# Attention probabilities turned by a DMA, and s_j laid along the rows through memory: a graph network on one core

## What is computed

```python
h = jnp.maximum(_layernorm(x, axis=-1), 0.0)
mask = adj + eye > 0
for l in range(3):
    si = h @ attn_w[l, :d]
    sj = h @ attn_w[l, d:]
    scores = si[:, :, None] + sj[:, None, :] + attn_b[l]
    scores = jnp.where(scores >= 0, scores, 0.2 * scores)
    scores = jnp.where(mask, scores, -jnp.inf)
    attn = jax.nn.softmax(scores, axis=-1)
    agg = jnp.einsum('bij,bjd->bid', attn, h)
    r = layernorm(h + agg, g1[l], beta1[l])
    ff = jax.nn.gelu(r @ W1[l] + b1[l], approximate=False) @ W2[l] + b2[l]
    h = layernorm(r + ff, g2[l], beta2[l])
out = x + h
```

## Time and profile before

| what | value |
|---|---|
| runs | 2316.35, 2315.44, 2313.62 us |
| median | 2315.44 us |
| the profiled execution | 2317.27 us, span 2315.5 us |
| PE busy | 2247.7 us, 97% of the span |
| PE weight loads busy | 1575.8 us, 68% |
| DVE busy | 1793.1 us, 77% |
| ACT busy | 1905.2 us, 82% |
| POOL busy | 1872.8 us, 81% |
| DMA, SP's queue | 101.37 MB, 19.3% of 16 engines |
| granted TensorE clock, mean | 0.992 |

### The profile page before, as it was taken

The page is one execution under the profiler, slowest core; times in us unless marked ns, Lnnn a source line. Parts: engine busy times, 40 slices in busy tenths (PEclk is TensorE's granted clock), DMA queues, the critical chain, the costliest instruction groups (busy, mean ns, idle before and its releaser), DMA issues.

```text
span 2315.5 us, 46432 instructions
## 1 busy us (share of the span) xinstructions
PE 2247.7 (97%) x15840; PEld 1575.8 (68%) x15840; DVE 1793.1 (77%) x5887; ACT 1905.2 (82%) x3496; POOL 1872.8 (81%) x1642
## 2 busy tenths in 40 slices
PE   4899999999999999999999999999999999999998
PEld 3666777776667677777666767777766677777675
DVE  7677777778887777777888877777888877777765
ACT  6778888888888888888888888888888888888874
POOL 6467877888988787878898878787989887878786
PEclk9899999999999999999999999999999999999999
DMA  6321111124442111112443111111443211111133
GB/s 180 91 65 28 24 24 24 24 42 83 96 105 47 20 28 19 29 21 53 101 100 88 33 20 28 19 29 19 83 105 88 46 24 24 26 22 28 38 69 78
DMA packets 279273, 120.06 MB, mean 52 GB/s; under 512 B 209792, under 2 KB 277376, under 8 KB 279040
## 3 DMA queue, kind: packets, MB, share of 16 engines
q1 hardware_dynamic: 263200, 101.37, 19.3%
q0 software_dynamic: 15840, 15.73, 4.6%
HBM read 49.96 MB, written 16.78 MB: 29 GB/s over the span
## 4 chain that ended last, share of the span: by engine, by line
PE 75%; DVE 12%; ACT 8%; issue 3%; DMA 1%; POOL 1%; SPq 0%; DVEq 0%; POOLq 0%; ACTq 0%
PE p_hid L417 34%; PE p_pair L431 33%; PE p_pair L477 4%; DVE g_lo L645 2%; DVE bn L652 2%; PE p_pair L455 2%; ACT probs L566 2%; PE p_pair L463 1%; DVE res L728 1%; ACT p_hid L531 1%; ACT L531 1%; DVE res L749 1%; ACT L566 1%; ACT g_hi L536 1%; DVE adj_in L673 1%
## 5 line engine op out<-in xcount | busy, mean ns | idle before, releaser
L645 DVE TENSOR_TENSOR g_lo<-p_hid,g_hi 128x512 f16<-128x512 f32 x768 | 529.9, 690 | 475.7 <-ACT g_hi L536 469.2
L431 PE MATMUL p_pair<-w_hi,g_hi 128*128 128x256 f16 x3072 | 837.9, 273 | 0.0
L431 PE MATMUL p_pair<-w_lo,g_hi 128*128 128x256 f16 x3072 | 837.8, 273 | 0.0
L431 PE MATMUL p_pair<-w_hi,g_lo 128*128 128x256 f16 x3072 | 837.8, 273 | 0.0
L531 ACT ACTIVATE p_hid<-p_hid,b_eff 128x512 f32<-128x512 f32 x768 | 505.5, 658 | 310.0 <-PE p_hid L417 308.3
L897 POOL TENSOR_TENSOR rstd<-var_eps,minus_half 128x4 f32<-128x4 f32 x224 | 236.6, 1056 | 382.9 <-DVE minus_mean L660 382.8
L536 ACT ACTIVATE g_hi<-p_hid 128x512 f16<-128x512 f32 x768 | 459.3, 598 | 24.5
L417 PE MATMUL p_hid<-hT_hi,w_hi 128*128 128x512 f16 x1536 | 458.2, 380 | 6.5 <-DMA hT_hi<-h_hi 3.5
L417 PE MATMUL p_hid<-hT_lo,w_hi 128*128 128x512 f16 x1536 | 458.7, 380 | 0.9 <-DMA hT_lo<-h_lo 0.8
L417 PE MATMUL p_hid<-hT_hi,w_lo 128*128 128x512 f16 x1536 | 458.6, 380 | 0.0
L431 PEld LDWEIGHTS p_pair<-w_lo,g_hi 128*128 128x128 f16 x3072 | 300.8, 98 | 106.7 <-issue 0.3
(11 more groups left out here) (73 smaller groups left out, 3520.2 us busy)
## 6 DMA issues: line engine op xcount, KB each, us to landing
x_in<-in_x SPq DMA_DIRECT2D x32, 512.0 KB, 3.8
out<-w_f SPq DMA_DIRECT2D x31, 512.0 KB, 5.0
w_f<-in_x POOLq DMA_DIRECT2D x30, 512.0 KB, 6.1
adj_in<-in_adj SPq DMA_DIRECT2D x32, 256.0 KB, 4.4
...
hT_hi<-h_hi SPq DMA_TRANSPOSE x96, 3.1
hT_lo<-h_lo SPq DMA_TRANSPOSE x96, 3.1
...
```

Of the source, the lines that this page charges most:

```text
L431: mm = pe.matmul(ff_banks(s)[:, t, :], g[i][:, nodes], w[l][:, c, :], start=(c == 0 and t % 2 == 0 and n == 0), stop=(c == C - 1 and n == ...
L645: dve.tensor_tensor(g_lo[i][:], p_hid[k][:], g_hi[i][:], ALU.subtract).then_inc(g_lo_ready, 1)
```

## The change

- `transpose_probs` and `copy_probs` go. ACT makes p_hi, a float16 copy of the probabilities, in SBUF; DVE makes p_lo = probs - p_hi, in SBUF; two DMA transposes on SP's queue write pT_hi and pT_lo.
- `spread_sj` on PE stays for the first four items only. From item 4 on SP writes s_j to a small DRAM buffer (`sj_to_memory`) and reads it back, repeated over the 128 partitions, as sj_rows in SBUF (`sj_to_rows`). The scores read sj_rows in place of the PSUM bank.
- The order in the slot changes on every engine: on DVE p_lo goes from chunk 4 to chunk 0, the feed residual from 2 to 1, its statistics from 3 to 2, the scores from 4 to 3, the attention residual from 7 to 5, the dots from 5 to 6, the mask from 6 to 7. ACT's exponentials go from 5 to 6 and the copy p_hi stands in 7. On POOL the norm after the feed moves to the slot after, before the layer's output. The folds for layers 1 and 2 stand as halves in chunks 3 and 4 of slots 1 and 3. Opening and loads of x are rearranged, and there is one more slot at the end.

```diff
+        sj_rows = sb("sj_rows", [P, T, N])
+        sj_memory = [nc.dram_tensor(f"sj_memory{i}", [T, N], F32).ap() for i in range(2)]
...
-        pT_hi, pT_lo = sb("pT_hi", [P, TN], F16), sb("pT_lo", [P, TN], F16)
+        p_hi, p_lo = sb("p_hi", [P, T, N], F16), sb("p_lo", [P, T, N], F16)
+        pT_hi, pT_lo = sb("pT_hi", [P, T, N], F16), sb("pT_lo", [P, T, N], F16)
...
+            def turn_probs_hi(r, s):
+                sp.wait_ge(p_hi_ready, total(r, s, 1, 1))
+                if later(r, s):
+                    sp.wait_ge(agg_ready, total(r, s - 1, 1, 1))
+                sp.dma_start_transpose(pT_hi[:], p_hi[:].rearrange("p t n -> p (t n)")).then_inc(pT_hi_ready, 16)
...
+            def sj_to_memory(r, s):
+                sp.wait_ge(dots_ready, total(r, s, 8, 8))
+                if later(r, s, 6):
+                    sp.wait_ge(sj_in, sj_total(r, s - 2))
+                with nc.allow_non_contiguous_dma("four bytes of each node and graph"):
+                    sp.dma_start(sj_memory[s % 2].rearrange("t n -> n t"), s_j[s % RING][:]).then_inc(sj_out, 16)
+
+            def sj_to_rows(r, s):
+                sp.wait_ge(sj_out, sj_total(r, s))
+                if later(r, s, 5):
+                    sp.wait_ge(score_steps, total(r, s - 1, 5, 4))
+                sp.dma_start(sj_rows[:].rearrange("p t n -> p (t n)"),
+                             sj_memory[s % 2].rearrange("t n -> (t n)").partition_broadcast(P)).then_inc(sj_in, 16)
...
-                    if c == 4 and is_item(r, s + 2):
-                        transpose_probs(r, s + 2)
+                    if c == 6 and is_item(r, s + 2):
+                        aggregate(r, s + 2)
                     if c < LAG and is_item(r, s - 1):
                         feed(r, s - 1, C - LAG + c)
                     if c >= LAG and is_item(r, s):
                         feed(r, s, c - LAG)
 
-                    if c == 3 and is_item(r, s + 3):
-                        spread_sj(r, s + 3)
-                    if c == 6 and is_item(r, s + 2):
-                        aggregate(r, s + 2)
...
-            def copy_probs(r, s):
-                act.wait_ge(pT_psum, total(r, s, 1, 1))
-                act.activation(pT_hi[:].rearrange("p (t n) -> p t n", n=N), pT_bank(s), ACT.Copy).then_inc(pT_hi_ready, 1)
+            def high_probs(r, s):
+                act.wait_ge(probs_ready, total(r, s, 4, 4))
+                if later(r, s):
+                    act.wait_ge(pT_hi_ready, total(r, s - 1, 16, 16))
+                act.activation(p_hi[:], probs[:], ACT.Copy).then_inc(p_hi_ready, 1)
...
             def add_scores(r, s):
                 q = s % RING
-                dve.wait_ge(sj_rows_ready, total(r, s, 1, 1))
+                first = isinstance(r, int) and r == 0 and s < 4
+                if first:
+                    dve.wait_ge(sj_rows_ready, s + 1)
+                else:
+                    dve.wait_ge(sj_in, sj_total(r, s))
+                rows = sj_bank(s) if first else sj_rows
                 dve.wait_ge(dots_ready, total(r, s, 8, 8))
                 if later(r, s):
                     dve.wait_ge(leaky_ready, total(r, s - 1, 2, 2))
                 for t in range(T):
-                    dve.scalar_tensor_tensor(out=scores[:, t, :], in0=sj_bank(s)[:, t, :], scalar=s_i[q][:, t:t + 1],
+                    dve.scalar_tensor_tensor(out=scores[:, t, :], in0=rows[:, t, :], scalar=s_i[q][:, t:t + 1],
                                              in1=mask[q][:, t, :], op0=ALU.add, op1=ALU.add).then_inc(score_steps, 1)
...
             def low_probs(r, s):
-                dve.wait_ge(pT_hi_ready, total(r, s, 1, 1))
-                dve.tensor_tensor(pT_lo[:].rearrange("p (t n) -> p t n", n=N), pT_bank(s),
-                                  pT_hi[:].rearrange("p (t n) -> p t n", n=N), ALU.subtract).then_inc(pT_lo_ready, 1)
+                dve.wait_ge(p_hi_ready, total(r, s, 1, 1))
+                if later(r, s):
+                    dve.wait_ge(pT_lo_ready, total(r, s - 1, 16, 16))
+                dve.tensor_tensor(p_lo[:], probs[:], p_hi[:], ALU.subtract).then_inc(p_lo_ready, 1)
...
-                if is_item(r, s - 2):
-
+
+                if is_item(r, s - 2) and not (isinstance(r, int) and (r, s) == (LOOPS, PER + 1)):
+                    norm_feed(r, s - 2)
                     layer_output(r, s - 2)
```

More of the change, by code:

```diff
@@ L55 @@
 LOOPS = ITEMS // PER - 1
[L56 removed]
+FOLD_AT = {4: 1, 6: 2}
 def layer_of(s):
@@ L131, in slots @@
             slot(r, s)
-    for s in range(FIRST_LOOP_SLOT, PER + 1):
+    for s in range(FIRST_LOOP_SLOT, PER + 2):
         slot(LOOPS, s)
@@ L285, in gnn_kernel, with sj_total, x_source @@
         pieces = [(l, n) for l in range(L) for n in range(4)]
-        act_pieces = dict(zip([(s, c) for s in range(4) for c in (0, 1)], pieces[4:]))
-        dve_pieces = dict(zip([(s, c) for s in range(3) for c in (5, 6)] + [(3, 2), (3, 3)], pieces[4:]))
+        act_pieces = dict(zip([(0, 6), (0, 7), (1, 0), (1, 3), (2, 0), (2, 3), (3, 0), (3, 3)], pieces[4:]))
+        dve_pieces = dict(zip([(0, 7), (1, 1), (1, 4), (2, 1), (2, 4), (2, 7), (3, 1), (3, 4)], pieces[4:]))
+        def sj_total(r, s):
+            return total(r, s, 16, 16 - 4 * 16)
+        def x_source(r, s):
+            return X[s] if isinstance(r, int) and r == 0 and s in (2, 3) else x_in[s % 2]
         block = ctx.enter_context(nc.Block())
@@ L317, in store, with turn_h_hi @@
                 sp.dma_start(graphs(out, g), y_out[g % 2]).then_inc(stored[g % 2], 16)
-            def turn_h(r, s):
-                i = s % 2
+            def turn_h_hi(r, s):
                 if later(r, s, 2):
                     sp.wait_ge(hid_psum, total(r, s - 2, C, C))
-                for h, hT, made, turned in ((h_hi, hT_hi, h_hi_ready, hT_hi_ready), (h_lo, hT_lo, h_lo_ready, hT_lo_ready)):
-                    sp.wait_ge(made, total(r, s, 1, 1))
-                    sp.dma_start_transpose(hT[i][:].rearrange("p t k n -> p (t k) n"),
-                                           h[:].rearrange("p t d -> p (t d)")).then_inc(turned, 16)
@@ L328, in slot, with turn_h_lo @@
-            def slot(r, s):
+                sp.wait_ge(h_hi_ready, total(r, s, 1, 1))
+                sp.dma_start_transpose(hT_hi[s % 2][:].rearrange("p t k n -> p (t k) n"),
+                                       h_hi[:].rearrange("p t d -> p (t d)")).then_inc(hT_hi_ready, 16)
+            def turn_h_lo(r, s):
+                sp.wait_ge(h_lo_ready, total(r, s, 1, 1))
+                sp.dma_start_transpose(hT_lo[s % 2][:].rearrange("p t k n -> p (t k) n"),
+                                       h_lo[:].rearrange("p t d -> p (t d)")).then_inc(hT_lo_ready, 16)
@@ new lines, in slot @@
+            def slot(r, s):
+                if is_item(r, s + 2):
+                    turn_probs_hi(r, s + 2)
+                if is_item(r, s + 3) and s >= 1:
+                    sj_to_rows(r, s + 3)
+                if is_item(r, s + 2):
+                    turn_probs_lo(r, s + 2)
+                if is_item(r, s + 3) and layer_of(s + 3) == 0 and group_of(r, s + 3) + 2 < G:
+                    sp.wait_ge(mask_steps, group_total(r, s + 3, 2, 2))
+                    load_adj(group_of(r, s + 3) + 2)
+                if is_item(r, s - 3) and layer_of(s - 3) == L - 1 and not (isinstance(r, int) and (r, s) == (LOOPS, PER + 1)):
+                    store(r, s - 3)
+                if is_item(r, s + 1):
+                    turn_h_hi(r, s + 1)
@@ L434, in feed, with fold_bias @@
                 mm.then_inc(ff_done, 1)
-            def fold_bias(l, bank):
+            def fold_bias(l, bank, half):
                 pe.wait_ge(w_dma[0], 16 * (l + 1))
                 pe.wait_ge(cols_dma, 2 * 16)
-                for c in range(C):
+                for c in range(C // 2 * half, C // 2 * (half + 1)):
                     for k in range(KD):
@@ L976, in slot @@
                     h_residual(r, s + 1)
-                if is_item(r, s - 1):
-                    inverse_deviation(s - 1, 2, total(r, s - 1, 10, 10), total(r, s - 1, 2, 1))
-                    if not (isinstance(r, int) and (r, s) == (LOOPS, PER)):
-                        norm_feed(r, s - 1)
             def first_deviation(i, n):
```

252 lines of the change are left out of this document (133 added, 119 removed).

## The result

The changed kernel takes **2567.5 us** (median of 4 runs, 2564.3 to 2571.0), the kernel before 2314.7 on the same chip: a ratio of 1.109, with a 95% interval of 1.108 to 1.111. It is slower, as forecast, but by 253 us and not by 160: 92 us beyond the forecast's 2475 and 27 beyond the end of the range. The profiled execution has a span of 2569.2 us.

What follows compares the result with a forecast made beforehand. TensorE's instruction list bounded the kernel before; after, VectorE's scores alternating with GpSimd make slots 24.9 us against TensorE's 22.2. Opening 169.6 + slots 2292 + end 13.5 = 2475 us; range 2210 to 2540, the likeliest case's own 2420 to 2540.

Steps and rivals of the forecast that it cites:

- What goes: On TensorE, both transposes leave, 2 x 0.44 = 0.87 us a slot, for a floor of 22.2 us.
- I take 4 ... and 3.1 for the read back. ... Cost 0: SP's queue: s_j's write 4 us and read back 3.1, back at 15.1 before scores start at 15.8; cost 0.
- The alternation: VectorE's two-SBUF-input scores take turns with GpSimd's h_lo and both h_res, one whole instruction each; slot 24.9 us against 22.2.
- The layer-0 slots, 25.4: 24 slots where VectorE also takes input statistics and the mask, which waits 0.95 and 1.1 us; 25.4 us each.
- The rival "s_j late": s_j's transfers end late, each us beyond 15.8 costing 1 us a slot; at 7.8 twice, 2624 us; chance 6%.
- TensorE stays the bound: Rival: VectorE passes the four short scores in one go; 2223 us, or 2257 if layer-0 slots wait; chance 28%.
- The moves priced at 0: p_hi replaces the copy pT_hi on ScalarE; norm_feed fills GpSimd's 4.12 us wait one slot later; each cost 0.
- The opening and the end: Opening left at 169.6 us, give or take 10; end 13.5: three feeds 3.9 and 9.6 from the last feed residual.
- p_lo about 1 us: Sign expected in the profile after: VectorE's p_lo, with both inputs in SBUF, takes about 1 us.
- The turned probabilities hidden: DMA turns of p_hi and p_lo cost nothing: p_lo ready about 9.6 us into VectorE's slot, read some 11 us later.

Runs made afterwards that it cites:

- e11_one_input: e4_wide with GpSimd's h_lo and both h_res as same-size instructions with one SBUF input, part of the result left out; 2251.4 us, 0.972 of the kernel before.
- e10_act_copy: e4_wide with ScalarE copying sj_rows into PSUM for the scores and the mask ahead of the attention residual; 2281.4 us, 0.985 of the kernel before.
- e12_mask_stats: e10_act_copy with the layer-0 items' mask made behind the attention residual and its statistics; 2232.6 us, 0.964 of the kernel before.
- e4_wide: Changed kernel with s_j memory laid out nodes by graphs, so the write is 128 pieces of 16 bytes; 2520.6 us, 1.089 of the kernel before.
- e1_static: Changed kernel with scores from item 4 on reading a constant in SBUF and no s_j transfers; 2507.9 us, 1.083 of the kernel before.
- e3_tensor: Changed kernel with s_j spread by four TensorE transposes into PSUM again, no transfer through memory; 2333.2 us, 1.007 of the kernel before.
- e5_order: Changed kernel with the turn of p_lo ahead of the s_j read back on SP's list; 2551.1 us, 1.102 of the kernel before.

## Why the prediction was wrong, point by point

- **What goes** (22.2 us a slot): right. e11_one_input, e10_act_copy and e12_mask_stats have ordinary slots of 22.1 to 22.2 us.
- **"I take 4 ... and 3.1 for the read back. ... Cost 0": the step that failed.** It is a term of the sum, mis-sized: 9.1 and 5.2 in the slot shown (8.7 to 12.2 over all slots for the first, median 4.9 for the second; the read back took 3.7 even in e4_wide). b_col, with six times the elements in 7.8 us, was the wrong neighbour: its small elements are read from memory, and here they are written to it side by side. The price: 47 us, the step from e4_wide to the changed kernel. With the write repaired the time, 2520.6, lies in the range that was given.
- **The alternation**: right, in kind and in size, for the ordinary slot: four scores 7.1 us, the slot 24.7 against 24.9. It is not what the profile after shows at first sight (scores of 0.54 us, not the 1 to 2 forecast), since lateness has taken its place; e1_static and e4_wide bring it out. TensorE's hidden matmuls wait 243.5 us for g_lo in e1_static, 2.6 in each of 92 slots, where 2 to 3 was forecast; in the changed kernel it is 69.2.
- **The layer-0 slots, 25.4**: a second term that was too small, by 1.4 us in 24 slots, 34 us. The mask and its wait were right (1.65 + 1.31 us after, 3.05 forecast). But GpSimd's output steps that wait for the mask put h_lo and h_res off as well, so the scores meet both h_res whole, where I had only the rest of the first and the second. In this stretch of e4_wide the four scores take 2.58, 2.50, 0.43 and 0.43 us, and GpSimd beside them:

```profile
1227.11 5.69 DVE L775 SCALAR_TENSOR_TENSOR scores<-sj_rows,s_i,mask 128x128 f32<-128x128 f32 x4
```

```profile
1226.66 2.85 POOL L976 TENSOR_TENSOR h_res<-norm,g_rows 128x1024 f32<-128x1024 f32 x1
1229.59 2.35 POOL L978 TENSOR_TENSOR h_res<-h_res,res_rows 128x1024 f32<-128x1024 f32 x1
```

- So 2475 + 34 - 13 (65 ordinary slots of 0.2 less) = 2496; e1_static has 2507.9. Of the 12 us between, some 4 are in the nine slots right behind the layer-0 ones, which take 25.1 to 25.3; the rest is not accounted for. e4_wide is another 13 above it, and 47 of lateness make 2567.5.
- **The rival "s_j late" (6%)** named the mechanism, and its place. Its price was too simple: 1 us a slot for each us beyond 15.8, counted on TensorE's 22.2. It took the alternation away and put lateness in its place, as if only one of them could be there. In the slot shown it would have given 21.6 + 3.1 = 24.7; the slot was 26.2, for the one score that is still held (1.6 us). The range should have held this case: the upper bound of the unknown cost, which I had worked out (2624), lay outside it, at a chance of 6% that one far row had to carry.
- **The clock**: the forecast takes TensorE at full speed, though it has it idle 2 to 3 us a slot. No run separates what the lower clock costs, so each step between two runs given here may hold some of it.
- **TensorE stays the bound (28%)**: wrong; its argument, that short instructions in a row slip through, is refuted by the scores of e1_static.
- **The moves priced at 0** (norm_feed a slot later, p_hi for the copy of pT_hi, the fold): right, as far as the ordinary slots of e3_tensor go, for they take the 22.6 us of TensorE's list with all of these in. **The opening and the end**: right. The fifth turn of h_hi goes out 3.6 us earlier than before (155.4 against 159.0) and the sixth 3.2 later (186.9 against 183.7), where the forecast left 10 either way, and the last feed residual starts at 2559.58, 9.6 before the span's end, as in the earlier trace rows.
- **p_lo about 1 us**: right, 0.99. **The turned probabilities hidden**: nearly. The turn of p_lo goes out 7 us after p_lo is ready, behind the read back, and costs some 16 us (e5_order).
